# Window attention on one core: the position bias as two fp16 products in front of the turned scores, in place of POOL's product behind the softmax's Exp

## What is computed

```python
shifted = jnp.roll(x, (-SS, -SS), axis=(1, 2))
...
attn = jnp.einsum('bhnd,bhmd->bhnm', _l2n(q), _l2n(k)) * scale
tbl = jax.nn.relu(REL_TABLE @ cpb_w1.T + cpb_b1) @ cpb_w2.T
rpb = 16.0 * jax.nn.sigmoid(tbl[REL_IDX].reshape(N, N, NH).transpose(2, 0, 1))
attn = attn + rpb[None]
...
attn = jax.nn.softmax(attn.reshape(-1, NH, N, N), axis=-1)
out = jnp.einsum('bhnm,bhmd->bhnd', attn, v).transpose(0, 2, 1, 3).reshape(-1, N, C)
```

## Time and profile before

| what | us |
|---|---|
| median of three runs | 3420.0 (3405.8 to 3424.6) |
| the profiled execution, its own time | 3387.5 |
| its span, first to last instruction | 3385.7 |
| TensorE, VectorE (DVE), ScalarE (ACT), GpSimd (POOL) busy | 2962.9, 2441.2, 1576.2, 1288.1 |
| mean granted TensorE clock | 0.879 |
| first and last Exp of the attention stage (L560), start | 99.2 and 966.2 |

### The profile page before, as it was taken

One profiled execution on the slowest core, in us unless ns is written; L12 is line 12 of the kernel. 1 busy time (PEld: TensorE's weight loads), 2 busy tenths in 40 slices (PEclk: granted clock), 3 DMA queues, 4 the chain that ended last, 5 costly groups with the idle time before them and its releaser, 6 DMA issues. The chain is left out here.

```text
span 3385.7 us, 93300 instructions
## 1 busy us (share of the span) xinstructions
PE 2962.9 (88%) x35559; PEld 2211.9 (65%) x35559; DVE 2441.2 (72%) x6382; ACT 1576.2 (47%) x3047; POOL 1288.1 (38%) x1360
## 2 busy tenths in 40 slices
PE   2899898889979979999888888888882999999999
PEld 1666666666657747777788666666662666666776
DVE  2676767877745558888677678877883677768888
ACT  1555545555524423433200333333330666777887
POOL 0444445555433321111000166666665000017776
PEclk9876767876669979999899989988985999999999
DMA  3000000000012210000000011111112444443333
GB/s 101 17 22 20 23 19 23 23 23 21 18 31 75 73 50 20 26 20 20 2 3 3 24 50 50 51 50 48 50 46 68 85 96 97 97 90 99 99 98 92
DMA packets 293305, 162.69 MB, mean 48 GB/s; under 512 B 93180, under 2 KB 284040, under 8 KB 292616
## 3 DMA queue, kind: packets, MB, share of 16 engines
q1 hardware_dynamic: 276488, 123.14, 13.5%
q0 software_dynamic: 16384, 33.59, 3.3%
HBM read 66.74 MB, written 71.30 MB: 41 GB/s over the span
## 5 line engine op out<-in xcount | busy, mean ns | idle before, releaser
L2302 DVE TENSOR_TENSOR e_glo<-e_g,e_ghi 128x512 f16<-128x512 f32 x540 | 375.1, 695 | 171.7 <-ACT e_ghi L2209 163.5
L2204 ACT ACTIVATE e_g<-psum,b 128x512 f32<-128x512 f32 x540 | 371.1, 687 | 181.7 <-PE psum L2358 164.4
L2188 POOL DMA_INDIRECT e_got<-ys_dram,e_idx x256 | 254.5, 994 | 508.9 <-DMA ys_dram<-e_yo 422.0
L2375 PE MATMUL psum<-w2hi,e_ghi 128*128 (+1 forms) x2160 | 394.7, 219 | 9.2 <-DVE e_glo L2302 7.0
L2379 PE MATMUL psum<-w2hi,e_glo 128*128 (+1 forms) x2160 | 390.1, 219 | 0.0
L2377 PE MATMUL psum<-w2lo,e_ghi 128*128 (+1 forms) x2160 | 390.1, 219 | 0.0
L503 POOL TENSOR_TENSOR pT<-pT,rpbx 128x1024 f32<-128x1024 f32 x128 | 300.7, 2349 | 27.9 <-ACT pT L560 27.9
L1738 POOL DMA_INDIRECT xs_dram<-m_xt,m_idxl x256 | 269.4, 1052 | 105.5 <-issue 72.3
L2375 PEld LDWEIGHTS psum<-w2hi,e_ghi 128*128 128x128 f16 x2160 | 210.8, 98 | 116.4 <-issue 44.9
L698 PE MATMUL psum<-vd,pT 128*64 128x18 f32 x4096 | 183.9, 237 | 62.1 <-ACT mT L565 62.1
L2377 PEld LDWEIGHTS psum<-w2lo,e_ghi 128*128 128x128 f16 x2160 | 211.2, 98 | 38.7 <-issue 0.3
(11 more groups left out here) (331 smaller groups left out, 7731.7 us busy)
## 6 DMA issues: line engine op xcount, KB each, us to landing
ys_dram<-e_yo SPq DMA_DIRECT2D x71, 256.0 KB
f_xm<-x_dram SPq DMA_DIRECT2D x32, 256.0 KB
mid_dram<-f_xm SPq DMA_DIRECT2D x32, 256.0 KB
l_t<-mid_dram SPq DMA_DIRECT2D x16, 512.0 KB
m_t<-mid_dram SPq DMA_DIRECT2D x16, 512.0 KB
res_dram<-m_rest SPq DMA_DIRECT2D x16, 512.0 KB
e_acc<-res_dram SPq DMA_DIRECT2D x32, 256.0 KB
out_dram<-e_acc SPq DMA_DIRECT2D x32, 256.0 KB, 2.2
```

The costliest lines, as they stand in the source:

```text
L2188: gp.indirect_dma_start(out=got[:, q % 2, k, t, :], out_offset=None, in_=ys, in_offset=bass.IndirectOffsetOnAxis(idx[:, q // 2, i:i + 1], 0))\
L2204: ac.activation(g32[:, c % 4, :], bank(c % 4), ACT.Gelu, bias=bias, scale=1.0 / WSCALE)\
L2302: ve.tensor_tensor(glo[:, c % 4, :], g32[:, c % 4, :], ghi[:, c % 4, :], ALU.subtract)\
L2375: pe.matmul(o, ghi[:, c % 4, g], w2hi[:, e, f, :], start=first and t == 0, stop=False, skip_group_check=True)
```

## The change

POOL's product and the semaphore pe_ok are dropped; sums(s-1) waits for pr_ok, the Exp, instead. Setup makes two fp16 tables in place of the fp32 exp table: rpb_hi = 16 sig rounded to fp16 (ACT, Copy in place of Exp), and rpb_lo = 16 sig - rpb_hi (two new DVE operations, which wait for ACT's seventh signal and stand in front of the splitting of w1). At the head of beat s TensorE gets `biases(s)`: for each of the two tables and each of the four banks one product of the fp16 identity (128x128) with 256 columns (128 of the table, repeated for the two windows), into the columns of the turned scores. The first four of the eight start the accumulation; the selector products of turned_scores(s) and scores(s+1), which start it today, no longer do. biases(s) waits for the Exp of pair s-1 and the maxima of pair s.

```diff
-                            ac.activation(rpbx[half].rearrange("q h n -> q n h"),
-                                          sig[half].rearrange("q n (h k) -> q n h k", k=2)[:, :, :, k], ACT.Exp, scale=16.0)\
+                            ac.activation(rpb_hi[half].rearrange("q h n -> q n h"),
+                                          sig[half].rearrange("q n (h k) -> q n h k", k=2)[:, :, :, k], ACT.Copy, scale=16.0)\
                                 .then_inc(s_ac, 1)
...
+                        ve.wait_ge(s_ac, 7)
+                        for k in range(2):
+                            half = slice(64 * k, 64 * k + 64)
+                            ve.scalar_tensor_tensor(out=rpb_lo[half].rearrange("q h n -> q n h"),
+                                                    in0=sig[half].rearrange("q n (h k) -> q n h k", k=2)[:, :, :, k], scalar=16.0,
+                                                    in1=rpb_hi[half].rearrange("q h n -> q n h"), op0=ALU.mult,
+                                                    op1=ALU.subtract).then_inc(s_ve, 1)
                         wd = 0
...
-                        if s.real():
-                            met(gp, pr_ok, s)
-                            p = pT[:, s.odd]
-                            e = rpbx[:].rearrange("p (j g) n -> p j (g n)", j=4).unsqueeze(2).to_broadcast([P, 4, 2, 2 * N])
-                            gp.tensor_tensor(p, p, e, ALU.mult).then_inc(pe_ok.sem, 1)
...
+                    def biases(q):
+
+                        met(pe, pr_ok, q - 1)
+                        met(pe, mx_ok, q)
+                        for part in (rpb_hi, rpb_lo):
+                            for j in range(4):
+                                pe.matmul(bank(j)[:, 256:512].rearrange("p (w n) -> p w n", w=2), ident16[:],
+                                          part[:, 2 * j:2 * j + 2, :].rearrange("p g n -> p (g n)").unsqueeze(1)
+                                          .to_broadcast([P, 2, 2 * N]), start=(part is rpb_hi), stop=False, skip_group_check=True)
+
                     def scores(q):
...
+                        alone = not (q - 1).real()
...
-                                                  high(kT[rows(j), q.u % 2, q.odd, half(w)]), start=True, stop=True)
+                                                  high(kT[rows(j), q.u % 2, q.odd, half(w)]), start=alone, stop=True,
+                                                  skip_group_check=True)
...
-                                              mT[rows(j), q.odd, :], start=(w == 0), stop=False, skip_group_check=True)
+                                              mT[rows(j), q.odd, :], start=False, stop=False, skip_group_check=True)
...
-                        met(pe, pe_ok, q)
+                        met(pe, pr_ok, q)
...
                     def beat(s):
+                        if s.real():
+                            biases(s)
                         if (s + 1).real():
                             scores(s + 1)
```

More of the change, by code:

```diff
@@ L188, in phase_setup @@
                 selk = keep("selk", [P, 4, 4, N], F16)
-                rpbx = keep("rpbx", [P, NH // 2, N])
+                rpb_hi = keep("rpb_hi", [P, NH // 2, N], F16)
+                rpb_lo = keep("rpb_lo", [P, NH // 2, N], F16)
                 vd = keep("vd", [P, 4, 4, NH // 2, 2, HD + 1])
@@ L340, in sb @@
                 return c1.enter_context(nc.sbuf_tensor(name, shape, dt))
-            wqkT, projT, g1, be1, qb2, pb2, msk, eps, mx2, selk, rpbx, vd = (
-                W[k] for k in "wqkT projT g1 be1 qb2 pb2 msk eps mx2 selk rpbx vd".split())
+            wqkT, projT, g1, be1, qb2, pb2, msk, eps, mx2, selk, rpb_hi, rpb_lo, vd = (
+                W[k] for k in "wqkT projT g1 be1 qb2 pb2 msk eps mx2 selk rpb_hi rpb_lo vd".split())
             xw = sb("xw", [P, NP, C])
@@ L369, in phase_attention @@
             stored = [psig(f"stored{p}", 1, 16) for p in range(NP)]
-            (s_ps, mx_ok, mT_ps, mT_ok, t_ps, pr_ok, pe_ok, o_ps, rs_ok, on_ok, onT_ps, onT_ok, v_ps, v_ok, pj_ps, st_ok, mv_ok, h_ok, ve_ok, rstd_ok,
+            (s_ps, mx_ok, mT_ps, mT_ok, t_ps, pr_ok, o_ps, rs_ok, on_ok, onT_ps, onT_ok, v_ps, v_ok, pj_ps, st_ok, mv_ok, h_ok, ve_ok, rstd_ok,
              xb_ok, x1_ok) = (psig(k) for k in (
-                 "s_ps mx_ok mT_ps mT_ok t_ps pr_ok pe_ok o_ps rs_ok on_ok onT_ps onT_ok v_ps v_ok pj_ps st_ok mv_ok h_ok ve_ok rstd_ok "
+                 "s_ps mx_ok mT_ps mT_ok t_ps pr_ok o_ps rs_ok on_ok onT_ps onT_ok v_ps v_ok pj_ps st_ok mv_ok h_ok ve_ok rstd_ok "
                  "xb_ok x1_ok").split())
```

## The result

The changed kernel takes 3464.6 us (median of four runs, 3452.0 to 3472.3) beside 3412.9 us before (four runs, one more than when I predicted, 3404.0 to 3424.6): the ratio is 1.0146, 95% interval 1.0097 to 1.0194. I had forecast 3374 us, range 3325 to 3455, with 0.67 on faster. The profiled execution of the changed kernel took 3472.3 us, span 3470.5.

What follows compares the result with a forecast made beforehand. TensorE was taken to bound the window-attention stage at 1.2 GHz, with its clock deciding. Profiled 3387.5 us minus 30 for the stage gave 3357, plus 17 for half the run difference 3374; range 3325 to 3455.

Steps and rivals of the forecast that it cites:

- The waits absorb nothing: Attention beats: the biases' 0.87 us moves the whole chain; the rival that waits absorb them, 3250 us, had chance 0.04.
- 12.3 to 13.5: Attention stage: double beats at 2.4 GHz forecast at 12.9 us; under 12.3 or over 13.5 would mean wrong.
- break-even clock: Attention stage: no gain or loss at 16% of the time at 1.2 GHz, a mean clock of 0.92.
- the forecast of the clock: Attention stage: biases make falls rare and short, mean clock 0.97, 6% at 1.2 GHz; chance 0.62 for 0.95 and up.
- the sign of being wrong: Attention stage: a clock staying under 0.92 would show the prediction wrong.
- 30 us less: Attention stage: one double beat per 13.2 us at the expected clock, 837 us instead of 867.
- The burst: Head of each attention beat: eight bias products at 0.109 us cost TensorE 0.87 us at 2.4 GHz.
- The setup: Before the attention stage: two extra DVE operations +1.4 us, at worst +2.5; together with the stage's end zero.
- The rule that I weighed: Attention stage: the clock falls only in idle gaps, so more products change nothing and cost their whole price.
- slower at today's mix: Attention stage: the clock keeps its pattern, 1011 us, 144 more; as a rival, chance 0.14.
- (b): Attention stage: in-between clock of 0.85 to 0.94, stage 855 to 916 us, total 3375 to 3469; chance 0.20.
- the 32.5: Whole kernel: median of three runs, 3420.0 us, lies 32.5 above the profiled time; half was expected to vanish.

Runs made afterwards that it cites:

- e1: Changed kernel without its eight bias products, so without position bias and POOL's product: attention stage, first to last Exp, 870 us at clock 0.70.
- e5: Changed kernel plus six dense idle products (result unread) in front of the sums of even beats: stage 841 us, ratio to before 0.995.
- e9: Changed kernel with only the four products of the high part, low part of the bias left out: stage 897 us at clock 0.80.
- e7: Changed kernel with the two DVE operations for the low part moved behind the splitting of w1: stage 899 us, ratio to before 1.010.
- e3: Kernel before plus dense 128x128 idle products in front of the sums, eight in even beats, three in odd: stage 771 us, ratio 0.975.
- e4: Kernel before plus as many idle products at the same places as e3, each on a 32x32 corner of the array: stage 847 us, clock 0.83.
- e10: Kernel before with only DVE's x1 update moved in front of the LayerNorm statistics, no idle work: stage 878 us at clock 0.69.
- e6: Changed kernel with the biases of the next pair moved in front of the sums: stage 806 us, ratio to before 0.986.
- e8: e3 with DVE's x1 update moved in front of the LayerNorm statistics: stage 737 us, ratio to before 0.966.
- e11: Changed kernel with biases in front of the sums (e6) and the low part made later in setup (e7): stage 812 us, ratio 0.979.

## Why the prediction was wrong

**Where it held.** TensorE is the bound, and the clock decides. The waits absorb nothing: 1.11 us in the even beat stays. POOL's product was worth only DVE's relief: double beats of 11.22 us in e1. Double beats of 13.26 us stayed inside the 12.3 to 13.5 that I had named. The biases do lift the clock, from 0.70 (e1) to 0.89. And the sign of the stage hung on a break-even clock.

**The step that failed: the forecast of the clock.** I wrote that the biases "stand exactly between the sums and the scores, in the hole before which the clock falls", and took 0.97. It came to 0.89, under the 0.92 that I had named as the sign of being wrong, and the term "30 us less" came out as 44.5 us more. The low-use stretch begins in front of the place that I chose: turned scores, a wait for ACT, sums. The biases stand behind it and closed only its end. In the kernel before, 14 of the 19 falls in the stage come behind the sums and the scores, in L726 at the head of the odd beat; in the changed kernel 24 of 26 come during the sums, earlier than the biases could help. My own row said so: the stretch before the fall in the earlier trace rows began with a wait, and the sums filled its middle. It is the even beat's hole alone: in both profiles every fall in the stage comes behind an even pair's Exp, and none behind the odd beat's sums, whose wait is 0.4 us in the changed kernel. e5 measures the error: 911 to 841 us, 70 us, from filling this hole alone. With the clock high throughout I had 819 us, and most of the difference from 841 is the price of the burst.

**Two sizes.** The burst: 0.87 us a beat taken, 1.02 measured (e1, e9), because entering and leaving it costs 0.14 us that a row of consecutive products does not show: 127 x 0.15 = 19 us, and it moves the break-even: with 13.26 and my 19.9 it is an estimated 9% of the time at 1.2 GHz, a clock of 0.96, in place of 16% and 0.92. The setup: zero taken, with 2.5 at worst, 8.5 measured (7 to 8 in the other profiles with this setup), and e7 takes it away. I priced an operation on every 64th element of an fp16 table from one with consecutive elements. That the stride makes the difference is the likeliest reason, but no run isolates it.

**The rule that I weighed.** The Trainium skill, page "TensorE: Matmul & The Clock Gate", section "Why this matters for your kernels", ties the fall of the clock to idle gaps. By it more products would change nothing. e3 and e4 fill the same waits equally and end at 0.98 and 0.83: the traces do not agree with it as a rule on gaps alone. The outcome that I drew from it, slower at today's mix, was right in sign and further off than mine in size: 1011 us, where 911 came.

**The chances.** What came is my case (b), with a clock at 0.89, plus the two sizes. By (b), 22% low time with 13.26 in place of 12.9 and the setup's 8.5 us would have been 909 + 8.5 in place of 867, so 3438 on the profiled time and 3471 with the 32.5: the measured 3465 lies within. It also lies in the interval that I gave (b), 3375 to 3469, but of (b)'s chance only 0.06 was for slower, and my range ended at 3455. The lower end of (b) was wrong as a sum: 3375 is 855 us with all of the 32.5 gone; with half of it gone it is 3392. With 0.62 on a clock above 0.95, from one fall and one rise looked at closely, I was too sure of where in the beat the fall stands.

## What to carry to other kernels

Where TensorE is the bound and its granted clock is under 1, first find the place in the loop at which it falls, and put dense work there: eleven idle products a double beat gave 2.5% here, while relieving the other engines (e1, e10) gave nothing by itself: the beats at 2.4 GHz were shorter, but there were no more of them (28 before, 25 in e1, 21 in e10, of 63). If work has to be added to TensorE, the place here was a wait, in front of the sums and not behind them: e6 differs from the changed kernel by this alone, and is 106 us faster in the stage. Price a strided write, and the entry and exit of a burst, from a row that has them.

## What the runs showed that I had not expected

- Adding work that nobody reads makes the kernel faster: 0.975, or 0.966 with the x1 update moved.
- Shorter beats did not shorten the stage: double beats from 12.15 to 11.2 us at 2.4 GHz came with a clock of 0.70 (e1) and 0.69 (e10) instead of 0.73. That is one profile each, and the same code gave 0.89 and 0.91 in two (changed, e7), so a cause for the lower clock is not shown.
- Some DVE operations of 0.2 to 0.34 us between SBUF tiles that start beside POOL's 128x1024 product last until that ends: 1.89 us for L613, ending 0.1 us after it (e8), as L601 did in the earlier trace rows (613.76 + 1.92 against 613.18 + 2.35). Not all do: in e8 the reduction L603, 128x512, starts beside the product in 60 beats and takes its 0.67 us each time, as the maxima from PSUM (L593) keep their 1.21.
- Writing fp16 with a stride of 64 elements, 64x512: 2.5 us on ACT with Copy (1.1 us for the fp32 table with the same stride, with Exp) and 2.5 us on DVE, which reads with that stride too.
- The same experts' stage takes 774 us in five of the profiles (before, changed, e9 to e11) and 975 to 991 us in the eight from the other two chips (e1 to e8), at a clock of 0.98 against 0.89 to 0.91. Why is open.
